# Expert loads and stores from ScalarE's queue, a second row buffer for the last batch, and two reordered table steps, in a fused transformer block on one core

## The chip, the core and the metric

One core of a Trainium2 chip runs the whole program in one launch. The engines are TensorE (PE in the rows), VectorE (DVE), ScalarE (ACT), GpSimd (POOL) and SyncE (SP, which only issues transfers here). The metric is the device time of one execution in microseconds. Three executions of the kernel before took 423.67, 422.94 and 422.52 us, median 422.94.

## The reference

The block has two halves on x of 4 batches by 512 tokens by 256 features, in float32:

```
mod = silu(c) @ wmod                       # per batch: sa, ca, ga, sb, cb, gb (256 each)
ga, gb = sign * max(|.|, 0.25)
h = layernorm(x) * (1 + ca) + sa
q, k, v = h @ wq + bq, h @ wk + bk, h @ wv + bv          # 16 heads of 16
scores = (q k^T) * gamma**(n - m) for n >= m, else 0      # retention, no softmax
ret = scores @ v, normed per head over (tokens, features), * gn_w + gn_b
x = x + ga * ((silu(h @ wg + bg) * ret) @ wo + bo)
h = layernorm(x) * (1 + cb) + sb
top 2 of 8 experts by h @ gate; weights = softmax over the two
x = x + gb * sum over the two of weight * (silu(h @ w0[e]) * (h @ w1[e])) @ wo[e]
```

Each expert has two 256x512 matrices and one 512x256. All outputs are returned as 4x512x256.

## The kernel before, in words

**Attention half.** A loop over the four batches (b = 0 to 3), unrolled, is written out once for each engine. For batch b TensorE does the projections q0, q1, k0, k1 (`project`), the value rows v01 and v23 (`rows_v`), the transposed keys (`rows_k`), the gate g0 and g1, the chunk states (`state_parts`), the scores of two sets of chunks (`scores(b, 0)` and `scores(b, 1)`), the products with the states (`from_states`), and transposes the next batch's x (`turn_x`). ScalarE takes results out of PSUM (`queries`, `keys`, `gate`, `features`), and VectorE masks the scores (`masks`) and adds. The second product with the values (`values(b, u)`) runs one batch later, between the projections. So do the per-head norm (`average`, `group_stats` to `group_scale`, `group_normed`), the product with the gate (`gated`), the output projection (`out_rows`, `attention_out`), the second layernorm (`second_normed`, written to the row buffer h2) and its transposes (`turn_h2`, `h2_features`). The router (`router`), its ranking (`rank`, `choose_top` to `rows_of_tokens`) and GpSimd's `scatter` of each token's row to DRAM run two batches later. Eight indirect transfers of 260 KB a batch write each token's row (features, weights, token number, gb) to the place of its two experts in `routed`.

PSUM results go through two rings. The front ring has four banks, so item i may be written when item i - 4 is drained: scores s03 of the last batch needs the bank of g0. The tail ring has two banks, with logits, rank, the table steps and the outputs in a fixed order of `tail_items`.

**Expert half.** 39 tiles of 128 rows, each of one expert. Tiles 0 to 8 (`EARLY`) hold rows of the first two batches alone and start while the last batch is still in its tail. Their table (which tile begins where, of which expert) is made in the last batch by `tiles_of_experts(0)`, `counts(0)`, `tiles_before(0)`, `firsts(0)`, `tile_columns(0)`, `fold(0)` and `table_rows(0)`. A second table for tiles 9 to 38 is made between tiles 4 and 8. Per tile TensorE does `turn_rows`, two products up (L1657 in the early tiles, L1666 to L1670 with split weights in the later ones), `turn_hidden` (L1678) and the product down (L1686), and GpSimd adds the rows to the output in DRAM (L633).

**Order and queues.** Every engine's instructions are in an order written by hand, and every cross-engine dependency is a semaphore. SP issues nearly all transfers in its own order: at the start the inputs, then per batch the two experts of that batch (`load_expert`, three transfers of 512 KB each) behind the end of `values(b - 1, 1)` (`pv_done`), the store of x of an earlier batch (`store_x`), ga, sb and cb rows, and the gb rows into h2 (`fill_gb`, which waits for the scatter of the batch before). In the tail `second_normed(3)` on ScalarE writes to the same h2 that the scatter of batch 2 reads, and waits for it (`scattered`), and `fill_gb(3)` on SP does too. The names on the rows: `h` is h2, `parts` holds q and the states, `kT` the keys, `sm` the masked scores and also ro and the tanh, `vx` the values with zeros between heads, `we` all eight experts' weights.

The lines below are those of the profile.

Of the kernel before, what the change touches and what calls it, by code (L numbers as in the profile page):

```python
# [21 lines left out]
F32 = mybir.dt.float32  # L22
F32R = mybir.dt.float32r
I32 = mybir.dt.int32
# [101 lines left out]
def adaln_block(nc, x, wq, bq, wk, bk, wv, bv, wg, bg, wo, bo, gn_w, gn_b, gamma,  # L126
                gate_k, w0, w1, wo_e, c, wmod, out):
    ctx = ExitStack()
    with ctx:
# [75 lines left out]
        h2 = sb("h2", [P, NC, ROW])  # L205
# [4 lines left out]
        tmpl = z[:, :, :].rearrange("p k n -> p (k n)")[:, 0:ROW]  # L210
# [4 lines left out]
        zeros, idch = h2[:, 0, 0:CH], h2[:, 1, 0:CH]  # L215
# [161 lines left out]
        def _(sp):  # L377
# [3 lines left out]
            def load_expert(e):  # L381
                for o, w, k, n in we_v:
                    sp.dma_start(we[:, e, o:o + k * n].rearrange("p (k n) -> p k n", k=k),
                                 w[e].rearrange("(k p) n -> p k n", p=P)).then_inc(we_in, 16)

# [28 lines left out]
            def store_x(b, done_sem):  # L414
                wait(sp, tail.drains(b, "wo23"))
                sp.dma_start(out_v[b], xs[:, b * NC:(b + 1) * NC, :]).then_inc(done_sem, 16)

            def fill_gb(b):

                if b:  # L420
                    sp.wait_ge(scattered, SCATTERS * b)
                sp.dma_start(h2[:, 0, GB:ROW], gb_dram[b].partition_broadcast(P)).then_inc(gb_rows, 16)


            for b in range(B):
                p = b - 1
                if b == 0:
                    sp.wait_ge(front.full, front.filled(b, "q0"))
                else:
                    sp.wait_ge(pv_done, SETS * b)  # L430
                if b == B - 1:
                    sp.wait_ge(gb_out, 16)
                load_expert(2 * b)
                load_expert(2 * b + 1)
                if p >= 0:
                    sp.wait_ge(front.full, front.filled(b, "g0" if b == B - 1 else "g1"))
                    if p >= 1:
                        store_x(p - 1, x2_out)
                    if b + 1 < B:
                        sp.wait_ge(x1_ready, b)  # L440
                        load_ga(b + 1)
                    if p >= 1:
                        sp.wait_ge(h2_ready, p)
                        load_sbcb(p)
                    fill_gb(p)
# [1325 lines left out]
```

## Time and profile before

| | |
|---|---|
| median of three executions | 422.94 us |
| profiled execution, its own time | 424.81 us |
| its span, first to last instruction | 423.1 us |
| mean granted TensorE clock | 0.937 |
| TensorE busy | 373.8 us (88%) |
| VectorE, ScalarE, GpSimd busy | 257.2, 171.5, 229.5 us |
| moved by DMA | 49.05 MB, mean 116 GB/s |

The span is what the rows speak of, and the rest of the profiled time lies around it. Busy time of TensorE is modelled from the issue of matmuls, so a granted clock of 0.5 shows as longer matmuls and not as idle time. The attention half takes about 172 us, the overlap of its tail with the early tiles goes on to about 250, and the rest is the loop over tiles.

### The profile page before, as it was taken

To read this page: it belongs to the slowest core of one execution; us is meant where nothing else is said; L and a number is where in the kernel's file an instruction comes from. 1 tells how busy PE (TensorE), PEld (TensorE's weight loads), DVE (VectorE), ACT (ScalarE), POOL (GpSimd) and SP (SyncE) were. 2 spreads that over 40 slices of the span, in tenths; PEclk is the share of its full clock that TensorE was granted. 3 is DMA by queue.
4 is the path that set the end of the run, shared out by engine and by line. 5 is a ranking of instruction groups with operands and counts; after the bars stand their busy time and mean duration, and the time that the engine had idled before them with its cause. 6 is when DMAs were issued, how large, how long until landed. Compare 5 with 4: busy or idle time off the path is not lost.

```text
span 423.1 us, 11448 instructions
## 1 busy us (share of the span) xinstructions
PE 373.8 (88%) x3889; PEld 278.0 (66%) x3890; DVE 257.2 (61%) x726; ACT 171.5 (41%) x262; POOL 229.5 (54%) x172
## 2 busy tenths in 40 slices
PE   3995899999889859887799899999999999999990
PEld 3464657776666537654476468888888888888870
DVE  6368317836833658673265566777777777777740
ACT  3514145463444311221331145555555555555530
POOL 3202520563754253617256457787777778777751
PEclk9998589999968988999699999999999999999997
DMA  6819007007900884217229844433333433433322
GB/s 226 273 34 317 4 24 279 28 2 258 323 24 3 282 294 119 52 52 252 53 42 285 245 84 75 78 75 75 75 75 75 75 75 75 75 75 76 51 25 25
DMA packets 32322, 49.05 MB, mean 116 GB/s; under 512 B 3198, under 2 KB 18972, under 8 KB 32284
## 3 DMA queue, kind: packets, MB, share of 16 engines
q1 hardware_dynamic: 23656, 34.60, 27.4%
q0 software_dynamic: 8176, 13.65, 14.6%
q8 instruction: 26, 0.43, 0.4%
q10 hardware_dynamic: 452, 0.28, 0.2%
q14 instruction: 12, 0.10, 0.1%
HBM read 30.35 MB, written 18.16 MB: 115 GB/s over the span
## 4 chain that ended last, share of the span: by engine, by line
PE 67%; issue 8%; DVE 8%; ACT 4%; DMA 4%; POOL 3%; SPq 2%; POOLq 0%; ACTq 0%; DVEq 0%
PE ps L1686 14%; PE ps L1391 9%; PE ps L1670 6%; PE ps L1667 6%; PE ps L1666 6%; PE ps L1678 3%; PE ps L1505 3%; PE ps L1657 3%; PE ps L1410 3%; PE ps L1444 2%; PE ps L1480 2%; DMA out_dram<-wg_s,qd 2%; POOL routed L591 2%; PE ps L1573 2%; PE ps L1465 1%
## 5 line engine op out<-in xcount | busy, mean ns | idle before, releaser
L623 POOL TENSOR_TENSOR w_lo<-we,w_hi 128x1024 fp32r<-128x1024 f32 x30 | 74.7, 2490 | 20.7 <-ACT w_hi L807 20.5
L1686 PE MATMUL ps<-we,qeo 128*128 x312 | 77.7, 393 | 6.6 <-ACT qeo L792 6.2
L1686 PEld LDWEIGHTS ps<-we,qeo 128*128 128x128 f32 x312 | 58.2, 193 | 25.1 <-issue 17.7
L633 POOL DMA_INDIRECT out_dram<-wg_s,qd x30 | 47.1, 1570 | 38.8 <-issue 15.8
L792 ACT COPY qeo<-ps 128x512 f32<-128x512 f32 x39 | 22.9, 586 | 105.1 <-PE ps L1678 105.1
L591 POOL DMA_INDIRECT routed<-h,idx x32 | 33.0, 1031 | 20.1 <-DVE idx L1131 11.2
L1292 DVE TENSOR_TENSOR w_halves<-we,w_halves 128x1024 fp32r<-128x1024 f32 x30 | 36.8, 1226 | 7.6 <-ACT w_halves L807 7.6
L1657 PE MATMUL ps<-we,xn 128*128 x72 | 36.5, 632 | 0.8 <-issue 0.8
L1272 DVE SCALAR_TENSOR_TENSOR sm<-sm,ps 128x512 f32<-128x512 f32 x39 | 26.5, 679 | 12.7 <-ACT sm L797 12.7
L1264 DVE CAST rT_halves<-ps 128x256 fp32r<-128x256 f32 x30 | 12.7, 424 | 33.2 <-PE ps L1573 33.2
L807 ACT CAST w_hi<-we 128x1024 fp32r x30 | 31.6, 1053 | 0.0
L807 ACT CAST w_halves<-we 128x1024 fp32r x30 | 31.4, 1048 | 0.2 <-issue 0.2
L1666 PE MATMUL ps<-w_halves,rT_halves 128*128 128x512 f32 x60 | 29.2, 487 | 0.0
L1279 DVE TENSOR_TENSOR sm<-sm,ps 128x512 f32<-128x512 f32 x39 | 26.5, 680 | 0.4
L1666 PE MATMUL ps<-w_hi,rT_halves 128*128 128x512 f32 x60 | 26.1, 435 | 0.0
L1017 DVE TENSOR_TENSOR sm<-ps,dmask 128x512 f32<-128x512 f32 x32 | 19.8, 681 | 9.1 <-PE ps L1444 9.1
L1678 PE MATMUL ps<-ident,sm 128*128 128x128 f32 x156 | 23.5, 273 | 0.3 <-DVE sm L1279 0.3
L736 ACT ACTIVATE h<-xs,nmr,rs 128x256 f32<-128x256 f32 x16 | 8.3, 590 | 37.9 <-POOL nmr L535 20.7
L1667 PE MATMUL ps<-w_halves,rT_halves 128*128 128x512 f32 x60 | 23.6, 394 | 0.0
L1667 PE MATMUL ps<-w_hi,rT_halves 128*128 128x512 f32 x60 | 23.6, 394 | 0.0
L797 ACT ACTIVATE sm<-ps 128x512 f32<-128x512 f32 x39 | 23.6, 604 | 0.0
L1678 PEld LDWEIGHTS ps<-ident,sm 128*128 128x128 f32 x156 | 19.1, 140 | 6.7 <-issue 2.1
(228 smaller groups left out, 725.2 us busy)
## 6 DMA issues: line engine op xcount, KB each, us to landing
rowbuf<-routed SPq DMA_DIRECT2D x39, 260.5 KB, 2.9
we<-in_ffn_w_kernel_dram SPq DMA_DIRECT2D x16, 512.0 KB
we<-in_ffn_wo_kernel_dram SPq DMA_DIRECT2D x8, 512.0 KB
routed<-z SPq DMA_DIRECT2D x9, 260.5 KB, 3.9
xs<-in_attn_x_dram SPq DMA_DIRECT2D x4, 512.0 KB, 11.7
out_dram<-xs SPq DMA_DIRECT2D x4, 512.0 KB, 3.1
we<-in_wmod_dram SPq DMA_DIRECT2D x1, 1024.0 KB, 10.0
sbcb<-gsc_dram SPq DMA_DIRECT2D x4, 256.0 KB, 5.8
```

Of the source, the lines that this page charges most:

```text
L591: g.indirect_dma_start(routed, bass.IndirectOffsetOnAxis(ap=idx[:, k, t:t + 1], axis=0), h2[:, t, :], None).then_inc(scattered, 16)
L623: g.tensor_tensor(w_lo[1], expert_up(e, 1), w_hi[1].bitcast(F32), ALU.subtract)\
L633: g.indirect_dma_start(out, bass.IndirectOffsetOnAxis(ap=meta[s % 4][:, TOK - D:TOK - D + 1].bitcast(I32), axis=0), ey[s % 2], None, compu ...
L807: a.copy(w_hi[which], expert_up(e, which)).then_inc(w_hi_ready[which], 1)
L1272: v.scalar_tensor_tensor(out=eth[s % 2], in0=eth[s % 2], scalar=1.0, in1=up_ps[s % 2][0][:, :], op0=ALU.add, op1=ALU.mult).then_inc(in_don ...
L1292: v.tensor_tensor(w_lo[0], expert_up(e, 0), w_hi[0].bitcast(F32), ALU.subtract)\
L1391: last = mm(front.bank(b, n)[:, :], s[:, k, ft * P:(ft + 1) * P], hT[:, k, :], start=k == 0, stop=k == FT - 1)
L1657: last = mm(up_ps[s % 2][which][:, :], rT[s % 2][:, k, :], weights(e, (which * FT + k) * F, F), start=k == 0, stop=k == FT - 1)
L1666: mm(dst, rT_hi[s % 2][:, k, :], w_hi[which][:, k * F:(k + 1) * F], start=k == 0, stop=False)
L1667: mm(dst, rT_lo[s % 2][:, k, :], w_hi[which][:, k * F:(k + 1) * F], start=False, stop=False)
L1678: last = tr(ps[5][:, k * P:(k + 1) * P], ein[s % 2][:, k * P:(k + 1) * P], ident[:, :])
L1686: last = mm(down_ps, eit[s % 2][:, k, :], weights(e, 2 * FT * F + k * D, D), start=k == 0, stop=k == KF - 1)
```

## The change

1. `load_expert` and `store_x` leave SP's queue and go to ScalarE's. Experts 0 and 1 are issued behind `keys(0, 1)`. In batch b >= 1 expert 2b is issued behind `queries(b, 0)` and expert 2b + 1 behind `keys(b, 0)`, with no wait for `pv_done`. `store_x(p)` is issued ahead of `h2_features(p)`, and that of batch 3 behind `act_step(2, 2)`.
2. The last batch gets a row buffer of its own, `h2_last`, at the address of vx (and the first 36 elements of z). `second_normed(3)` and `fill_gb(3)` no longer wait for `scattered`. `fill_gb(3)` moves up behind the loads of tile 1's rows. A wait for all scatters is new ahead of the first split weights (`weights_hi(9)`), which are written over vx, and `gb_copies(3)` waits for `prod_ready`.
3. In the last batch TensorE's `counts(0)` goes behind the projection k1, and VectorE's `tiles_before(0)` behind `group_stats`.
4. VectorE's `tile_columns(0)` goes ahead of `gated`.

```diff
@@ buffers
-        h2 = sb("h2", [P, NC, ROW])
+        h2_first = sb("h2_first", [P, NC, ROW])
+        h2_last = nc.alloc_sbuf_tensor_at("h2_last", [P, NC, ROW], F32, offset=offset["vx"])
+        spill = (NC * ROW - 2 * NC * D)
+        tmpl = z[:, :, :].rearrange("p k n -> p (k n)")[:, 2 * spill:2 * spill + ROW]
+        h2 = [h2_first, h2_first, h2_first, h2_last]
...
@@ SP
             def fill_gb(b):
 
-                if b:
+                if b == B - 1:
+                    sp.wait_ge(pv_done, SETS * B)
+                elif b:
                     sp.wait_ge(scattered, SCATTERS * b)
...
-            for b in range(B):
+            for b in range(1, B):
                 p = b - 1
-                if b == 0:
-                    sp.wait_ge(front.full, front.filled(b, "q0"))
-                else:
-                    sp.wait_ge(pv_done, SETS * b)
-                if b == B - 1:
+                sp.wait_ge(pv_done, SETS * b)
+                if b + 1 < B:
+                    sp.wait_ge(x1_ready, b)
+                    load_ga(b + 1)
+                if p >= 1:
+                    sp.wait_ge(h2_ready, p)
+                    load_sbcb(p)
+                if p == 0:
                     sp.wait_ge(gb_out, 16)
-                load_expert(2 * b)
-                load_expert(2 * b + 1)
...
@@ SP, early tiles
                 if i == 1:
-                    store_x(B - 2, x2_out)
                     sp.wait_ge(h2_ready, B - 1)
                     load_sbcb(B - 1)
-                if i == 3:
-                    store_x(B - 1, x2_last)
-                if i == 4:
                     fill_gb(B - 1)
@@ ScalarE
                 act.wait_ge(shift2, b + 1)
-                if b:
+                if 0 < b < B - 1:
                     act.wait_ge(scattered, SCATTERS * b)
...
                 queries(b, 0)
+                if b == B - 1:
+                    act.wait_ge(gb_out, 16)
+                if b:
+                    load_expert(2 * b)
                 if p >= 1:
                     top_tanh(p - 1)
...
                 keys(b, 0)
+                if b:
+                    load_expert(2 * b + 1)
                 keys(b, 1)
+                if b == 0:
+                    load_expert(0)
+                    load_expert(1)
...
+                    store_x(p)
+                if p >= 0:
                     if p == 0:
                         act.wait_ge(mod2_ready, 2)
                     h2_features(p)
...
             act_step(2, 2)
+            store_x(b)
             h2_features(b, [0])
@@ VectorE
                         tiles_of_experts(0)
+                    group_stats(p)
+                    if last:
                         tiles_before(0)
-                    group_stats(p)
...
                 rows_v(b, "v23", 2)
+                if last:
+                    tile_columns(0)
                 if p >= 0:
                     gated(p)
@@ TensorE
                     values(p, 1)
+                project(b, "k", wk_s, 1)
                 if final:
                     counts(0)
-                project(b, "k", wk_s, 1)
```

Three places where the instructions of an engine stand otherwise. The first is VectorE in the last batch, from the last value rows to the chunk states; `sm<-sm,z` is the product with the gate, `stc` to `done` the tile columns. Before:

```order
L967 TENSOR_TENSOR vx<-ps,bv_bc 128x8x2x16 x2
L1056 TENSOR_TENSOR sm<-sm,z 128x512 x2
L1168 TENSOR_SCALAR stc<-ps 8x1
L1174 TENSOR_TENSOR enc<-stc,tls 8x1
L1175 SCALAR_TENSOR_TENSOR bas<-stc,base 8x1
```

and after, with the tile columns' last operation directly ahead of the gate product:

```order
L1175 TENSOR_SCALAR stc<-ps 8x1
L1181 TENSOR_TENSOR enc<-stc,tls 8x1
L1182 SCALAR_TENSOR_TENSOR bas<-stc,base 8x1
L1184 TENSOR_SCALAR tile_i<-tile_f,stc 8x39
L1185 SCALAR_TENSOR_TENSOR bas<-done,bas 8x1
L1187 SCALAR_TENSOR_TENSOR ine<-tile_f,enc,tile_i 8x39
L1189 TENSOR_SCALAR row<-tile_f,bas 8x39
L1190 TENSOR_TENSOR tab<-row,ine 8x39
L1191 TENSOR_SCALAR tab<-ine,ecol 8x39
L1194 TENSOR_SCALAR done<-stc 8x1
L1195 SCALAR_TENSOR_TENSOR done<-done,tls 8x1
L1063 TENSOR_TENSOR sm<-sm,z 128x512 x2
```

All eleven operations of the tile columns are now ahead of the two gate products.

The second is ScalarE in the last batch, from the queries of tile 0 to the keys of tile 1 (with the waits at the rows' ends). Before:

```order
L694 ACTIVATE parts<-ps,vcol 128x512 [waits front_full]
L696 ACTIVATE qeo<-ps,bqp,par 128x8x64 x2
L745 ACTIVATE vt<-vd 128x4 [waits vd_ready]
L694 ACTIVATE parts<-ps,vcol 128x512 [waits front_full]
L696 ACTIVATE qeo<-ps,bqp,par 128x8x64 x2
L702 ACTIVATE kT<-ps,vcol 128x512 [waits front_full] x2
```

and after:

```order
L679 ACTIVATE qeo<-ps,bqp,par 128x8x64 x2
L730 DMA we<-in_ffn_w_kernel_dram 128x2x512 [waits gb_out]
L730 DMA we<-in_ffn_w_kernel_dram 128x2x512
L730 DMA we<-in_ffn_wo_kernel_dram 128x4x256
L739 ACTIVATE vt<-vd 128x4 [waits vd_ready]
L677 ACTIVATE parts<-ps,vcol 128x512 [waits front_full]
L679 ACTIVATE qeo<-ps,bqp,par 128x8x64 x2
L685 ACTIVATE kT<-ps,vcol 128x512 [waits front_full]
L730 DMA we<-in_ffn_w_kernel_dram 128x2x512 x2
L730 DMA we<-in_ffn_wo_kernel_dram 128x4x256
L685 ACTIVATE kT<-ps,vcol 128x512 [waits front_full]
```

Six transfers stand between activations that PSUM banks wait for.

The third is ScalarE at the early tiles 1 and 2, where `h` is the row buffer, L797 the tanh of a tile and L792 the copy of its hidden rows. Before:

```order
L797 ACTIVATE sm<-ps 128x512 [waits in_done,up0_full]
L736 ACTIVATE h<-xs,nmr,rs 128x256 [waits scattered,shift2]
L736 ACTIVATE h<-xs,nmr,rs 128x256 x3
L792 COPY qeo<-ps 128x512 [waits dn_full,it_full]
L797 ACTIVATE sm<-ps 128x512 [waits in_done,up0_full]
L727 ACTIVATE hT<-ps,modT 128x512 [waits tail_full]
```

and after:

```order
L802 ACTIVATE sm<-ps 128x512 [waits in_done,up0_full]
L719 ACTIVATE h_last<-xs,nmr,rs 128x256 [waits shift2]
L719 ACTIVATE h_last<-xs,nmr,rs 128x256 x3
L797 COPY qeo<-ps 128x512 [waits dn_full,it_full]
L802 ACTIVATE sm<-ps 128x512 [waits in_done,up0_full]
L735 DMA out_dram<-xs 128x4x256 [waits tail_dve]
L710 ACTIVATE hT<-ps,modT 128x512 [waits tail_full]
```

The order of the activations is the same, the wait for `scattered` is gone from the norm, and the store of batch 3 is new.

## Rows read from the trace of the kernel before

**Rows 1.** Windows table; busy us of each engine, clock, DMA share, GB/s.
```profile
38.00:42.00 4.00, 2.21 (x90) 1.79 (x76) 3.62 (x7) 0.00 (x0) 0.80 (x2) 0.56 0.95 330
114.00:118.00 4.00, 0.86 (x55) 0.72 (x49) 3.72 (x11) 0.00 (x0) 3.18 (x4) 0.87 0.63 218
151.00:157.00 6.00, 1.63 (x72) 1.32 (x64) 2.67 (x8) 0.00 (x0) 3.94 (x4) 0.80 0.89 305
...
204.00:210.00 6.00, 6.00 (x13) 3.73 (x14) 1.86 (x3) 0.14 (x1) 0.96 (x1) 0.57 0.22 61
```
**Rows 2.** Chain of waits; start us, us, what.
```profile
40.21 3.25 issue
...
114.78 3.14 issue
...
152.49 4.37 issue
...
170.79 0.69 issue
```
**Rows 3.** Windows between restarts; columns of rows 1 (matmuls, weight loads first).
```profile
43.45:117.92 74.46, 68.77 (x1394) 49.40 (x1395) 41.81 (x132) 31.12 (x52) 33.70 (x30) 0.89 0.39 132
117.92:130.44 12.52, 11.93 (x253) 10.03 (x253) 3.99 (x19) 7.09 (x12) 7.92 (x5) 0.76 0.05 14
130.44:156.84 26.41, 19.42 (x380) 12.57 (x379) 14.94 (x65) 7.20 (x12) 10.67 (x11) 0.89 0.66 222
156.84:167.87 11.02, 10.53 (x253) 8.34 (x254) 8.40 (x22) 0.95 (x2) 2.23 (x3) 0.79 0.45 134
167.87:171.47 3.61, 2.71 (x128) 2.21 (x127) 0.89 (x2) 2.57 (x5) 3.39 (x4) 1.00 0.02 5
```
**Rows 4.** The page's DMA queues; packets, MB, share.
```profile
q8 instruction: 26, 0.43, 0.4%
```
**Rows 5.** Timeline of SP's queue; start us, us, line.
```profile
30.03 0.94 SPq L383 DMA_DIRECT2D we<-in_ffn_w_kernel_dram  x2
...
137.96 1.76 SPq L383 DMA_DIRECT2D we<-in_ffn_w_kernel_dram  x2
...
148.85 0.39 SPq L416 DMA_DIRECT2D out_dram<-xs  x1
```
**Rows 6.** Expert loads by line (ns min/median/max), then ScalarE's timeline with its idle time.
```profile
L383 SPq DMA_DIRECT2D we<-in_ffn_w_kernel_dram x16: 368/489/1475, 30.0 to 140.8; - x16
...
31.90 0.69 ACT L708 ACTIVATE z<-ps,vcol 128x512 f32<-128x512 f32 x1 [8.34 <-PE ps L1391]
...
134.48 0.69 ACT L694 ACTIVATE parts<-ps,vcol 128x512 f32<-128x512 f32 x1 [4.57 <-PE ps L1391]
```
**Rows 7.** Timeline of the last batch; start us, us, instruction [idle before <-releaser].
```profile
139.17 0.20 PE L1545 MATMUL ps<-ident,carry_early 128*8 128x1 f32 x2 [1.24 <-DVE base L1142]
...
149.33 0.14 DVE L1168 TENSOR_SCALAR stc<-ps 8x1 f32<-8x1 f32 x1
149.45 0.69 ACT L708 ACTIVATE z<-ps,vcol 128x512 f32<-128x512 f32 x1 [1.79 <-DVE sm L1056]
...
149.62 1.48 PE L1426 MATMUL ps<-vx,xn 64*32 64x32 f32 x112 [0.80 <-DVE stc L1168]
...
151.55 0.15 DVE L1188 SCALAR_TENSOR_TENSOR done<-done,tls 8x1 f32<-8x1 f32 x1
```
**Rows 8.** Timeline from the down product of tile 0 on.
```profile
192.41 1.89 PE L1686 MATMUL ps<-we,qeo 128*128 x8
...
194.03 0.20 POOL L535 TENSOR_TENSOR nmr<-nm,rs 128x4 f32<-128x4 f32 x1
...
201.10 2.07 ACT L736 ACTIVATE h<-xs,nmr,rs 128x256 f32<-128x256 f32 x4 [9.35 <-DMA routed<-h,idx]
...
203.80 3.78 PE L1686 MATMUL ps<-we,qeo 128*128 x8 [5.42 <-ACT qeo L792]
...
207.37 2.77 PE L1657 MATMUL ps<-we,xn 128*128 x4
```

More of the change, by code:

```diff
@@ L412, in _ @@
             load_ga(1)
-            def store_x(b, done_sem):
-                wait(sp, tail.drains(b, "wo23"))
-                sp.dma_start(out_v[b], xs[:, b * NC:(b + 1) * NC, :]).then_inc(done_sem, 16)
             def fill_gb(b):
-                if b:
+                if b == B - 1:
+                    sp.wait_ge(pv_done, SETS * B)
+                elif b:
                     sp.wait_ge(scattered, SCATTERS * b)
-                sp.dma_start(h2[:, 0, GB:ROW], gb_dram[b].partition_broadcast(P)).then_inc(gb_rows, 16)
-            for b in range(B):
+                sp.dma_start(h2[b][:, 0, GB:ROW], gb_dram[b].partition_broadcast(P)).then_inc(gb_rows, 16)
+            for b in range(1, B):
                 p = b - 1
-                if b == 0:
-                    sp.wait_ge(front.full, front.filled(b, "q0"))
-                else:
-                    sp.wait_ge(pv_done, SETS * b)
-                if b == B - 1:
-                    sp.wait_ge(gb_out, 16)
-                load_expert(2 * b)
-                load_expert(2 * b + 1)
[L435 to L445, printed above, removed]
+                sp.wait_ge(pv_done, SETS * b)
[6 more added lines that the diff above has]
+                if p == 0:
+                    sp.wait_ge(gb_out, 16)
+                fill_gb(p)
             def load_rows(i, s):
@@ L740, in gb_copies, with load_expert, store_x @@
                 act.wait_ge(gb_rows, 16 * (b + 1))
-                a.copy(h2[:, 1:NC, GB:ROW], h2[:, 0:1, GB:ROW].broadcast_to([P, NC - 1, D])).then_inc(gb_copied, 1)
+                if b == B - 1:
+                    act.wait_ge(prod_ready, FT * B)
+                a.copy(h2[b][:, 1:NC, GB:ROW], h2[b][:, 0:1, GB:ROW].broadcast_to([P, NC - 1, D])).then_inc(gb_copied, 1)
+            def load_expert(e):
+                for o, w, k, n in we_v:
+                    act.dma_start(we[:, e, o:o + k * n].rearrange("p (k n) -> p k n", k=k),
+                                  w[e].rearrange("(k p) n -> p k n", p=P)).then_inc(we_in, 16)
+            def store_x(b):
+                wait(act, tail.drains(b, "wo23"))
+                act.dma_start(out_v[b], xs[:, b * NC:(b + 1) * NC, :]).then_inc(x2_last if b == B - 1 else x2_out, 16)
             def top_tanh(b):
@@ L1237, in _ @@
                     first_stats(1)
-                if last:
-                    tile_columns(0)
                 states(b)
@@ L1514, in turn_h2 @@
                     for t in range(NC):
-                        last = tr(tail_bank(b, n)[:, t * P:(t + 1) * P], h2[:, t, ft * P:(ft + 1) * P], ident[:, :])
+                        last = tr(tail_bank(b, n)[:, t * P:(t + 1) * P], h2[b][:, t, ft * P:(ft + 1) * P], ident[:, :])
                     last.then_inc(tail.full, 1)
```

21 lines of the change are left out of this document (9 added, 12 removed).

## The prediction, made before the changed kernel was run

> **What bounds the kernel now.** I read the page first for the shape: TensorE is busy 88% of the span and granted a mean clock of 0.937, so no other engine is near the bound, and what can be won is time in which TensorE stands still or runs at half its clock. Then the windows table, which says where that is. In three stretches of 4 to 6 us TensorE is busy for a fifth to somewhat over a half of the time, 38 to 42 and 114 to 118 in the middle of the attention part and 151 to 157 in the last batch; a fourth, 204 to 210, is busy throughout but at a granted clock of 0.57, near the lower level of 1.2 GHz (0.5) [rows 1]. That one follows a wait of 5.4 us that ends at 203.80 [rows 8]. The second half (expert tiles from about 250 us on) is a steady loop of about 5.3 us a tile with TensorE busy throughout. The change leaves that loop alone, so I look for the shift at which the loop is entered.
>
> The chain of waits shows what the first three stretches are: pieces called "issue" of 3.25, 3.14 and 4.37 us, in which TensorE waited for nothing that the profile shows [rows 2]. Each lies within a run of like small matmuls (from_states or scores), whose waits are all at its first instruction. A fourth such piece, 0.69 us, lies in values(3, 1). The counts between them say what they have in common: from one restart to the next TensorE issued 1394+1395, 253+253, 380+379, 253+254 and 128+127 matmuls and weight loads, each a little short of 11, 2, 3, 2 and 1 times 256 [rows 3] (a few per cent of records and the other instructions make up the rest). So TensorE stops at the end of a fixed-size block of its program and goes on when the next block is there. The page has a DMA queue for instructions, 26 packets with 0.43 MB, 16.5 KB a packet [rows 4]: the blocks come over the same 16 DMA engines as the data. Where the DMA share was 0.95, 0.63 and 0.89 [rows 1] the piece was 3.1 to 4.4 us, and where it was 0.02 it was 0.7 us [rows 2, 3]. I take the block's packet to stand behind whatever transfers are already queued. The Trainium skill (Runtime: NRT & Kernel Launch, Instruction fetch mechanics) says that instructions are refilled in 16 KiB blocks of 256 by a DMA queue of the sequencer, and that the cost of a boundary is "mostly hidden". The trace agrees on the block; the "mostly hidden" it contradicts at these three places, and by that rule the change would win nothing there (rival B).
>
> What was queued then is in SP's own order: expert weights, 3 MB a batch, from 30.03 and again from 137.96, and a 512 KB store of x at 148.85 [rows 5]. Batches 1 and 2 have the like.
>
> **The change, part by part.** Sums are made against the profiled execution: span 423.1, run 424.81, which is 1.87 above the median of 422.94. I subtract the sum from the median.
>
> (1) Experts 0 and 1 move from SP, behind the modulation rows, to ScalarE behind keys(0, 1). ScalarE has then nothing to do for 8.34 us (its next activation is at 31.90) [rows 6]. Six issues by 0.49 us, the median, are 2.9 us, and by the longest, 1.475, 8.9 us [rows 6]: hidden in all but the worst case, which would add 0.5. The 3 MB start at about 23.6 instead of 30.0, and are over at about 34 or 35 instead of 42 at this case's 350 to 380 GB/s. TensorE's next dense run starts at 37.2, so the stop of 3.25 us at 40.21 goes: gain 3.3. What is late next is the half clock, granted from 38.5 to 55 before. It came with the idle 34.3 to 37.1, which stays. I price it at nothing, and a faster return at up to 2.2 more (3.8 us of q0 projection at half speed). Lower end of this part: 0.
>
> (2) In batches 1 to 3 each expert is issued behind queries(b, 0) or keys(b, 0), and the x stores of batches 0 to 2 one stage later. That is 18 loads and 3 stores in ScalarE's order. Behind a load wait queries(b, 1), keys(b, 1) and the tanh for the weights. ScalarE sits idle 4.57 us before queries(3, 1) [rows 6], and in other batches the gaps there are 2 us or a little more, against three issues of 0.5 to 0.8 us each, so I cost it at nothing, up to 2 us in all. The second stop (3.14, batch 2): experts 4 and 5 now start some 6 and 3 us earlier and the store is gone from 109, so only the scatter of batch 0, paced by GpSimd at 1.27 us a piece, is left in flight. The stop shrinks to the uncongested 0.7 or less: gain 2.7. With no clock drop behind it (0.5 to 123.7) the 64 scores matmuls and eight transposes that took half speed come back by about 1: I take 0.6 of it. Sum 3.3, ends 0 and 4.5.
>
> (3) Last batch. counts(0) moves behind the k1 projection: TensorE's wait of 1.24 us for VectorE [rows 7] is covered by the projection, and VectorE starts the group statistics 0.9 us earlier without the four operations of tiles_before, so that average(2) comes 0.8 earlier: gain 0.8. tile_columns(0), from 149.33 to 151.70, 2.37 us [rows 7], now stands ahead of the gating product. So the firsts column is drained 1.8 us earlier, and state_parts doesn't wait its 0.80 us. But gate(3, 0) on ScalarE, which waits for the product (1.79 us already) [rows 7], starts 2.4 us later, and scores(3, 0) need its bank. They begin at about 153 instead of 151.1. That is where the stop of 4.37 us was: by then the experts (issued from 129 and 137 instead of 138) are over and the store is gone, so the block is there. scores end at 154.3 instead of 157.5. Then VectorE is late next: the table's rows, the gate product and four masks (some 3.9 us in all) end at 158.2, and the residual sum behind them, held by out_rows at half clock until 161.65 before, starts 3.4 earlier. TensorE, which comes to values(3, 0) early, runs into the block period that the trace shows undisturbed, 3.61 us from 167.87 to 171.47 [rows 3]: boundaries at 159.6, 163.2 and 166.8 instead of 164.8, 167.87 and 171.47, so values(3, 1) end 4.6 earlier. I take 4.2, between VectorE's 3.4 and TensorE's 4.6; ends 1.0 (if the stop stays) and 6.
>
> (4) The last batch's rows get a buffer of their own. second_normed(3) no longer waits for the scatter of batch 2, only for shift2, ready at 194.24 instead of 201.10 [rows 8]. turn_back(1) follows it, so ScalarE copies at 196.5 instead of 203.08. TensorE's down(1) then starts when its own projection ends, 198.4 instead of 203.80: 5.4. Without the idle the clock doesn't fall: down(1) takes 1.89 instead of 3.78, and the 2.77 of the next up part 1.88, 2.4 together up to the transposes at 209.98 [rows 8]. SP no longer waits for the scatter before fill_gb(3), so row 5 comes earlier. What is late next is GpSimd: its first accumulation lands at about 205 and the fifth tile's meta copy needs it, which costs at most 1. The new store sits in front of h2_features, 0.4 us, while ScalarE waits. The new wait of the first split weights for all scatters comes 9 us behind the last of them and is hidden. Gain 7.4, ends 4 and 8.1.
>
> Sum: 3.3 + 3.3 + 4.2 + 7.4 = 18.2, so 422.9 - 18.2 = 404.7; I say 405.
>
> A second rule of the Trainium skill speaks against (1) and (2): DMA: Bandwidth & Descriptors, "Issuing engines are not separate DMA queues", says that DMAs of all engines share the same 16 and that another issuer only saves issue time. The rows agree in that SP's issues cost nothing here: what is won is not by the other queue but by the earlier start.
>
> **Rivals.**
> A, the forecast: about 405 (399 to 410).
> B, the stops stay or move. If the block packets are late for another reason, or the expert bursts now catch the blocks fetched under values(0, 1) and values(1, 1), only (4) and the reorder of (3) remain. For it: the burst of batch 1 starts within a microsecond of a block boundary (11 blocks lie between 43.45 and 117.92), and 1.5 MB take 4.5 us. Against it: the boundaries after that have 5 us or more to the next. Time: 422.9 - 7.4 - 1.0 = 414.5, and 411 to 418 with one of the stops gone.
> C, the late gate decides. scores(3, 0) wait so long that the clock falls and out_rows stays slow, and GpSimd is the bound after 205. Part 3 gives 1, part 4 gives 5: 422.9 - 3.3 - 3.3 - 1 - 5 = 410.3, in A's or B's range.
> D, slower. ScalarE's queue blocks. If the ring is full, each of the 22 issues (18 loads, 4 stores) in its order takes the longest time seen on SP, 1.48 us, and all of it lies on the path of queries, keys and gates: 32.6 - 18.2 = 14.4, so 437. It decides above 18.2 / 22 = 0.83 us exposed per issue. For it: on SP the second load of a burst took that long. Against: idle of over 4 us beside most of them.
> E, the change doesn't do what it says: second_normed(3) is held by something that comes as late as the scatter, as its shift2 is computed on GpSimd between two pairs of scatters. The trace has it at 194.24, so little speaks for it: 422.9 - 10.8 = 412.1.
>
> **Chances.** A 0.58, B 0.22, C 0.08, E 0.03, D 0.05, and 0.04 for a sum near nothing. The range that should hold 8 in 10 goes down to 399 (part 1 with the clock back, part 2 and 3 at their ends) and up to 415, which takes in C, E and most of B. 0.3% is about what a measurement of this kernel can tell from no change, 1.3 us: faster 0.92, same 0.02, slower 0.06.
>
> **What would show it.** In the windows of the changed kernel the DMA burst of the first experts lies at 24 to 35, and no "issue" piece of over 1 us is left inside from_states(0), from_states(2) and scores(3, 0). ScalarE waits less than 1 us for anything behind a load. gate(3, 0) starts about 2 us after its old place relative to the product's operands. second_normed(3) is released by GpSimd's nmr, not by a DMA, TensorE's wait before down(1) is under 1 us and the clock beside it 1.00. The tile loop keeps 5.3 us. I am wrong if an "issue" piece of 2 us or more stands in values(0, 1) or values(1, 1), or if queries(b, 1) start later than before relative to their matmul.

## The result and the profile after

The changed kernel takes 405.25 us (median of 4 executions, 403.61 to 409.28), the kernel before 423.07 (4, 422.52 to 423.67). The ratio is 0.958, 95% interval 0.952 to 0.965: 17.8 us faster, against 18.2 forecast. A later series gave 405.79 (6 executions, 402.61 to 408.86). The trace below is of the execution that took 409.28, the slowest, with a span of 407.6; the others had spans of 401.9 to 403.6, so a part of what it shows is not in all of them. The medians here take in every execution; the ratios with an interval leave out those more than 1.5% above the fastest of their kernel.

The page of the changed kernel, queues and chain by engine:

```profile
PE 366.4 (90%) x3889; PEld 271.3 (67%) x3890; DVE 259.6 (64%) x726; ACT 171.3 (42%) x262; POOL 228.9 (56%) x172
...
q10 hardware_dynamic: 11140, 14.96, 10.7%
q8 instruction: 26, 0.43, 0.4%
...
PE 72%; DVE 8%; issue 6%; DMA 4%; ACT 4%; SPq 2%; POOL 1%; POOLq 0%; ACTq 0%; DVEq 0%
```
TensorE is busy for 7 us less, ScalarE's queue (q10) carries the 15 MB of experts and stores, and the instruction queue is the same [rows 4]. The chain of waits of the changed kernel (start us, us, what; "issue" is time in which TensorE waited for nothing that the profile names) answers to [rows 2]:

```profile
40.25 1.11 issue
...
90.72 1.10 issue
...
155.40 0.85 issue
158.89 0.98 issue
```
The piece in from_states(0) has fallen from 3.25 to 1.11 us. There is a new one of 1.10 in values(1, 1), and none in scores(3, 0). TensorE's timeline (idle before in brackets) shows the stretch around the first stop, the second stop and the last batch:

```profile
37.94 1.20 PE L1452 MATMUL ps<-qeo,kT 32*64 32x128 f32 x64 [2.34 <-ACTq L696]
...
42.34 1.62 PE L1452 MATMUL ps<-qeo,kT 32*64 32x128 f32 x64
...
109.44 1.18 PE L1473 MATMUL ps<-qd,parts 32*32 32x64 f32 x60
111.40 1.06 PE L1473 MATMUL ps<-qd,parts 32*32 32x64 f32 x52 [0.79 <-issue]
...
122.18 0.66 PE L1488 MATMUL ps<-sm,vx 64*32 64x64 f32 x27 [0.57 <-issue]
...
143.73 2.02 PE L1452 MATMUL ps<-qeo,kT 32*64 32x128 f32 x64 [2.73 <-ACTq L696]
```
The stop of batch 2 is 0.79 instead of 3.14. The block restart in values(2, 0) that stood at 130.44 [rows 3] comes at 122.18. In the last batch the 64 scores matmuls run through, but TensorE waited 2.73 us for the late gate first, and the 64 took 2.02 us, against 1.20 for the same count at 37.94: they ran at a granted clock of 0.50 instead of 1.00.

Around the routed rows of the last batch (timeline, for [rows 8]):

```profile
180.45 1.89 PE L1694 MATMUL ps<-we,qeo 128*128 x8
...
182.09 0.20 POOL L518 TENSOR_TENSOR nmr<-nm,rs 128x4 f32<-128x4 f32 x1
...
182.33 2.08 ACT L719 ACTIVATE h_last<-xs,nmr,rs 128x256 f32<-128x256 f32 x4 [2.54 <-POOL nmr L518]
...
186.26 1.89 PE L1694 MATMUL ps<-we,qeo 128*128 x8
```
second_normed(3) is released by GpSimd's nmr, down(1) waits for nothing and takes 1.89 instead of 3.78. Up to here TensorE is 17.5 us ahead of before (186.26 against 203.80). Then a part is given back. These are windows from down(2) to down(12), the changed kernel's first, then those of before:

```profile
195.15:259.37 64.22, 59.80 (x252) 41.52 (x252) 40.76 (x113) 21.51 (x33) 39.37 (x25) 0.95 0.52 130
```
```profile
215.43:275.26 59.83, 57.50 (x253) 40.24 (x252) 38.50 (x113) 21.64 (x33) 35.92 (x24) 1.00 0.55 137
```
The same ten tiles take 4.4 us longer, at a mean clock of 0.95 instead of 1.00. From down(12) on the shift stays: 15.9 us there, 15.5 at the end of the span.

### The profile page after: what moved, and what is told of

Its sections match the earlier page's. It is cut to its first block, busy times and chain, and to the rows that moved or that the text cites. A ratio compares the mean times of both kernels' runs of the same rounds, so it can differ in the third digit from the quotient of the medians.

```text
span 407.6 us, 11447 instructions
## 1 busy us (share of the span) xinstructions
PE 366.4 (90%) x3889; PEld 271.3 (67%) x3890; DVE 259.6 (64%) x726; ACT 171.3 (42%) x262; POOL 228.9 (56%) x172
## 4 chain that ended last, share of the span: by engine, by line
PE 72%; DVE 8%; issue 6%; DMA 4%; ACT 4%; SPq 2%; POOL 1%; POOLq 0%; ACTq 0%; DVEq 0%
PE ps L1694 14%; PE ps L1399 10%; PE ps L1675 6%; PE ps L1674 6%; PE ps L1678 6%; PE ps L1665 5%; PE ps L1513 4%; PE ps L1686 3%; PE ps L1488 3%; PE ps L1418 3%; PE ps L1581 2%; DMA out_dram<-wg_s,qd 2%; PE ps L1531 2%; DVE sm L1024 2%; PE ps L1452 2%
## 5 line engine op out<-in xcount | busy, mean ns | idle before, releaser
L1694 PE MATMUL ps<-we,qeo 128*128 x312 | 75.9, 386 | 1.1 <-ACT qeo L797 0.8
L797 ACT COPY qeo<-ps 128x512 f32<-128x512 f32 x39 | 22.9, 587 | 109.2 <-PE ps L1686 109.0
L574 POOL DMA_INDIRECT routed<-h_first,idx x24 | 24.7, 1030 | 16.2 <-DVE idx L1138 9.4
L1399 PE MATMUL ps<-hT,wq_s 128*128 128x512 f32 x32 | 21.3, 809 | 2.0 <-ACT hT L669 1.8
L530 POOL TENSOR_TENSOR qd<-parts,qdec 128x512 f32<-128x512 f32 x8 | 9.5, 1183 | 21.1 <-ACT parts L677 21.1
```

The source lines that it names most:

```text
L1399: last = mm(front.bank(b, n)[:, :], s[:, k, ft * P:(ft + 1) * P], hT[:, k, :], start=k == 0, stop=k == FT - 1)
L1694: last = mm(down_ps, eit[s % 2][:, k, :], weights(e, 2 * FT * F + k * D, D), start=k == 0, stop=k == KF - 1)
```

## Experiments

All times are medians; the kernel before ran beside each series and had 422.59 (19 executions, 412.60 to 439.35), 421.05 (11) and 421.50 (11). With that scatter, differences between two variants under some 2 us are not settled by the medians. The traces show where a wait stands and how long it is, but each is of one execution, and two traces of the same kernel differ too. Parts are numbered as in the prediction: 1 the loads of batch 0, 2 those of the other batches and the stores, 3 the reordering, 4 the buffer. In the edits, "..." marks what is left out.

**The two halves.** Only the last batch's buffer (part 4):

```diff
-        h2 = sb("h2", [P, NC, ROW])
+        h2_first = sb("h2_first", [P, NC, ROW])
...
+        h2_last = nc.alloc_sbuf_tensor_at("h2_last", [P, NC, ROW], F32, offset=offset["vx"])
...
+        h2 = [h2_first, h2_first, h2_first, h2_last]
```

> The kernel before with only the last batch's row buffer (h2_last over the values, gb_copies and fill_gb(3) at their new places); loads, stores, counts and tile columns stand as before. Theory: the wait of second_normed(3) for batch 2's scatter (5.42 us before router(3)) goes, and with it the half clock behind it, while 1 to 4 us come back in the tile tables and row loads behind the routing: 415 to 418 us, 5 to 8 faster than before; the stops at 40, 114 and 152 us stay at 3.2, 3.1 and 4.4 us. Rival (the gain of the whole change is in the queues alone, and the wait is replaced by another one in front of router(3)): 421 to 423 us.

417.62 us, 5.0 below before, span 415.7 against 423.1. Its stops stay at 4.03, 2.86 and 3.52 us. down(2) starts at 206.81, 8.6 earlier than before, and down(12) at 267.75, 7.5 earlier. The theory holds, with 417.62 in its range of 415 to 418; about 1 us is given back here between down(2) and down(12).

Only the queues (parts 1 and 2):

```diff
-                load_expert(2 * b)
...
-                        store_x(p - 1, x2_out)
...
+                if b:
+                    load_expert(2 * b)
...
+                    store_x(p)
```

The removed lines are SyncE's, the added ones ScalarE's. With them gone, SyncE's ga, sb and cb rows come earlier too.

> The kernel before with only the expert loads and the stores moved from SyncE to ScalarE; buffer, counts and tile columns as before. Theory: stops at 40 and 114 us fall to about 1 us, a new one of about 1 us comes in values(1,1), the stop in scores(3,0) shrinks or stays at up to 4.4 us since the batch's late part is as before: 411 to 417 us, 6 to 12 faster than before. Rival (ScalarE's queue pays for the issues, about 1.5 us each where it is waited for, so the loads alone bring nothing): 420 to 425 us. Second rival (the stops depend on the place in the program, not on what lies on the DMA engines): all three stops stay at 3 to 4 us, and the time is within 1 us of before.

409.98 us, 12.6 below before in the medians; the ratio is 0.973 (0.963 to 0.982), which is 7.5 to 15.7 us. That is the upper end of the 6 to 12 expected. TensorE's timeline of this kernel:

```profile
38.06 3.33 PE L1465 MATMUL ps<-qd,parts 32*32 32x64 f32 x112
...
46.06 1.98 PE L1391 MATMUL ps<-hT,wq_s 128*128 128x512 f32 x4 [1.00 <-ACT hT L665]
...
139.65 1.42 PE L1444 MATMUL ps<-qeo,kT 32*64 32x128 f32 x61
142.70 0.43 PE L1444 MATMUL ps<-qeo,kT 32*64 32x128 f32 x3 [1.63 <-issue]
...
178.02 1.89 PE L1686 MATMUL ps<-we,qeo 128*128 x8
...
200.91 1.97 PE L1686 MATMUL ps<-we,qeo 128*128 x8
```
No stop at all in from_states(0), and the following four projection matmuls at full clock (1.98 us) where before and the changed kernel took 3.78 and 3.51. But the 112 products took 3.33 us, where the changed kernel's two pieces took 1.18 and 1.05: the clock had fallen ahead of them instead. From the first scores matmul on it was 0.60 in the mean (window):

```profile
36.68:40.90 4.22, 4.21 (x162) 3.64 (x166) 3.36 (x6) 0.00 (x0) 1.58 (x2) 0.60 0.01 4
```
 The stop in scores(3, 0), which I had given to the reordering, is already 1.63 instead of 4.37 without it. The scatter's 5.42 us wait before down(1) is there as before.

**Queue or moment.** The changed kernel with SyncE issuing the expert loads at ScalarE's moments (the stores stay on ScalarE; shown for batches 1 to 3):

```diff
+                wait(sp, front.drains(b, "q0"))
...
+                load_expert(2 * b)
+                wait(sp, front.drains(b, "k0"))
+                load_expert(2 * b + 1)
```

> The changed kernel, except that SyncE issues the expert loads, at the moments of the batch at which ScalarE issued them (it waits for the drained banks of k1 in batch 0, of q0 and k0 in the others); the stores stay on ScalarE. Theory (what counts is when the loads' bursts stand against the block fetches, and not the queue that issues them): within 1.5 us of the changed kernel, 404 to 407 us, stops as in its chain (1.1 us at 40, 1.1 us at 91). Rival (ScalarE's own queue is the gain, because SyncE keeps its loads of ga, the shift rows and gb behind the waits): 410 to 417 us, with waits for those rows. Second rival (the issues on ScalarE cost it time): 401 to 403 us.

407.38 us (402.85 to 409.50), as good as the changed kernel (402.61 to 409.28), though a little above the 404 to 407 expected; the ratio to before is 0.961 (0.949 to 0.972), against 0.958. So for the expert loads the gain is the moment, not the queue. The rule of the Trainium skill that I weighed (DMA: Bandwidth & Descriptors, "Issuing engines are not separate DMA queues") says that a transfer runs on the same DMA engines whichever engine issues it, and this run agrees. The pieces are not all those of the changed kernel's chain: the first is 2.40 us instead of 1.11, and none stands at 91. What made the first longer is looked at below.

**Is a stop a block boundary?** The kernel before with 32 more TensorE instructions in the setup (each transpose is a weight load and a matmul):

```diff
+            for _ in range(16):
+                tr(ps[6][:, 0:P], ident[:, :], ident[:, :])
```

> The kernel before with 16 extra transposes of the identity on TensorE in the setup, into a bank that is overwritten later, so that every later matmul stands 32 instructions further on in TensorE's program. Theory (a stop is TensorE waiting for its next block of 256 instructions, fetched behind the expert bursts): the stops stay in the program's rhythm, so they move 16 matmuls ahead: in from_states(0) to behind some 46 matmuls instead of 62, in scores(3,0) to behind some 45 instead of 61; lengths of 2 to 5 us as before, total 421 to 426 us. Rival (the stops belong to what stands at that place, a bank or an operand): they stay behind the same matmuls, 62 and 61.

Timeline of before (for the counts), then of the shifted kernel:

```profile
38.32 1.89 PE L1465 MATMUL ps<-qd,parts 32*32 32x64 f32 x62
43.46 1.70 PE L1465 MATMUL ps<-qd,parts 32*32 32x64 f32 x50 [3.25 <-issue]
45.09 2.92 PE L1444 MATMUL ps<-qeo,kT 32*64 32x128 f32 x64
...
151.06 1.43 PE L1444 MATMUL ps<-qeo,kT 32*64 32x128 f32 x61
156.85 0.69 PE L1444 MATMUL ps<-qeo,kT 32*64 32x128 f32 x3 [4.37 <-issue]
```
```profile
38.25 0.94 PE L1467 MATMUL ps<-qd,parts 32*32 32x64 f32 x46
39.34 1.29 PE L1467 MATMUL ps<-qd,parts 32*32 32x64 f32 x66
...
143.63 1.08 PE L1446 MATMUL ps<-qeo,kT 32*64 32x128 f32 x45
148.51 1.11 PE L1446 MATMUL ps<-qeo,kT 32*64 32x128 f32 x19 [3.79 <-issue]
```
In scores(3, 0) the stop is behind 45 matmuls instead of 61, exactly 16 ahead, and nearly as long. In from_states(0) the break is behind 46 as expected, but it is no stop any more. In from_states(2) it is behind 44 instead of 60, with 1.23 us instead of 3.14, and a stop of 2.39 us stands ahead of it at 101.60, in the gate projection. So the places follow the count of TensorE's instructions, and the lengths follow what is under way there. The Trainium skill has such a boundary "mostly hidden" (Runtime: NRT & Kernel Launch, Instruction fetch mechanics); the 3.79 us here contradict it for dense small matmuls beside full DMA engines. Total 419.20, 3.4 below before in the medians, but the ratio is 1.002 (0.985 to 1.019), so the time has not changed; I had expected 421 to 426.

The traces also hold the start and the duration of every DMA packet, and the queue q8 of [rows 4] is TensorE's: this kernel has 27 packets on it instead of 26. In the kernel before the packets run from 40.92 to 42.00, 115.46 to 116.40 and 154.56 to 155.44 us, each inside one of the three stops, and TensorE starts again 1.46, 1.52 and 1.41 us behind their ends. Between 20 and 172 us the fourteen traces have 107 "issue" pieces ahead of TensorE's matmuls: 95 of them end 1.2 to 1.6 us behind the end of such a packet. The other twelve stand ahead of an up product or of out_rows(3), 3.0 us or more behind a packet, so they are waits of another kind. The queue's rows in the DMA view of before (packets, MB, share), over 40.90 to 41.00, 115.40 to 115.50 and 154.50 to 154.60 us, in which the three packets start:

```profile
q8 instruction: 1, 0.02, 68.0%
...
q8 instruction: 1, 0.02, 58.6%
...
q8 instruction: 1, 0.02, 55.4%
```
This shows what the stops are: the packet itself takes about 1 us, as elsewhere, but it starts late. That other transfers delay its start follows from the runs in which these were moved.

How late can be read as well. Where small matmuls follow and the DMA engines are free, the next packet starts 1.05 to 1.14 us behind the block's first matmul (43.46 to 44.51, 167.87 to 168.97, 171.48 to 172.62). With 1.0 for the packet and 1.4 behind it, a block takes 3.5 us, while its 128 small matmuls take 1.5 to 2.4 at full clock. That is the period of 3.61 us in [rows 3], and a remainder of about 1 us is left in such a run even when nothing holds the packet. In the changed kernel the packet of from_states(0) starts at 39.06, 1.12 us behind the first scores matmul at 37.94, so nothing held it, and the 1.11 us left are this remainder. With the queues alone it starts 1.02 us behind (36.68 to 37.70): there the block was in time because TensorE, at the lower clock, came to the boundary later. In the run with SyncE's early loads it starts 2.27 us behind (37.62 to 39.89), and the piece is longer by about as much. In the kernel before it starts 3.72 us behind (37.20 to 40.92), in the shifted one at 36.92, ahead of the scores.

**What held the block of batch 2.** The kernel before with experts 4 and 5 loaded in batch 1:

```diff
-                load_expert(2 * b)
-                load_expert(2 * b + 1)
+                if b != 2:
+                    load_expert(2 * b)
+                    load_expert(2 * b + 1)
+                if b == 1:
+                    load_expert(4)
+                    load_expert(5)
```

> The kernel before with experts 4 and 5 loaded by SyncE right behind 2 and 3 in batch 1, and no expert load in batch 2; all else as before. Theory (the packet of the block stood behind these loads): the stop in from_states(2) falls from 3.14 to 0.7 to 1.1 us and the clock there stays full, the stops at 40 and 152 us stay over 3 us, and nothing else moves much: 417 to 421 us. Rival (the store of x and the scatter, which stay where they are, hold the packet): the stop stays at 2.5 to 3.2 us.

The rival came out, a shade above its 2.5 to 3.2 us. Timeline and a window of this kernel:

```profile
117.39 1.17 PE L1469 MATMUL ps<-qd,parts 32*32 32x64 f32 x60
121.81 1.71 PE L1469 MATMUL ps<-qd,parts 32*32 32x64 f32 x52 [3.25 <-issue]
```
```profile
114.00:120.00 6.00, 4.56 (x135) 3.71 (x134) 5.14 (x15) 1.08 (x2) 4.16 (x6) 1.00 1.02 290
```
With no expert load in batch 2 the DMA engines are still full from 114 to 120, the block's packet starts only at 119.48, and the stop is 3.25 us. SyncE issued the store of x, the ga and the shift rows there from 112.77 on, beside the scatter. Which of these transfers alone would do it was not tried. A new stop of 2.67 us stands at 81.44, behind the doubled burst of batch 1. The time is of only two executions (417.77 and 428.39) and says nothing.

**The reordering.** The changed kernel once more, then without part 3:

> The changed kernel once more, unaltered, as the yardstick for the three kernels that run beside it. 403 to 409 us as measured before, and 16 to 19 below the kernel before.

```diff
-                if last:
-                    tile_columns(0)
...
+                if last:
+                    tile_columns(0)
...
-                project(b, "k", wk_s, 1)
                 if final:
                     counts(0)
+                project(b, "k", wk_s, 1)
```

> The changed kernel without its third part: counts(0), tiles_before(0) and tile_columns(0) stand at their old places; loads and stores on ScalarE and the buffer of the last batch as changed. Theory (formed after the two halves, 5.0 and 12.6 us below before, already made up the whole gain of 17.8): the queues had already shortened the stop in scores(3,0) from 4.37 to 1.63 us, so the reordering is worth 0 to 1.5: 404 to 408 us, within 1.5 of the changed kernel beside it. Rival (the prediction's term 3 at its full size): 4 us slower than the changed kernel, 409 us. In its trace I expect an issue piece of 1.0 to 2 us in scores(3,0) and no 2.7 us wait of TensorE for the gate.

405.79 (15.3 below before, a little under the 16 to 19 expected) and 407.87: 2.1 apart in the medians, with scatters of 402.6 to 408.9 and 401.6 to 411.6. The ratios to before, 0.964 (0.958 to 0.969) and 0.965 (0.956 to 0.973), do not tell them apart, so no gain of the reordering is shown. Its two halves taken back one at a time, tile_columns(0) behind the gate first, then counts(0) ahead of k1:

> The changed kernel with tile_columns(0) back behind the gating product; counts(0) behind k1 as changed. Theory (the columns delay gate(3,0) by some 2.4 us, TensorE waits 2.7 us for it and its clock falls, while the stop that the delay was to cover is over): scores(3,0) start 2 us earlier and an issue piece of 0.5 to 2 us comes back in them, together 0 to 2 us faster than the changed kernel beside it. Rival (the earlier block boundary is worth more than the gate): 1 to 3 us slower.

> The changed kernel with counts(0) back ahead of the k1 projection and tiles_before(0) ahead of group_stats(2); tile_columns(0) stays ahead of the gating product. Theory (no reorder at all cost 2.1 us and the columns alone gave 1.0 back, so the counts are worth about 3): 407.5 to 409.5, with the 1.24 us wait of TensorE for the base back. Rival (the 3 us are scatter between executions, the counts are worth the 0.8 us of the prediction): 405.5 to 407.

404.82 and 404.87 (the second in another series): neither alone costs anything that can be seen. With the columns behind the gate a piece of 1.52 us stands in scores(3, 0) again, and the 2.73 us wait for the gate is gone, as expected. With the counts back, TensorE's wait for the base is 0.46 us and not the expected 1.24. The 3 us that I expected of the counts did not show in the time, as the rival had it. What remains of the reordering is 0 to 2 us.

**Where the last 4 us went.** Timeline of the changed kernel, SyncE and TensorE:

```profile
206.18 9.83 SPq L456 DMA_DIRECT2D routed<-z  x8
...
217.36 15.75 SPq L439 DMA_DIRECT2D rowbuf<-routed  x4
...
219.69 0.29 PE L1573 MATMUL ps<-tab,ones 8*1 8x78 f32 x2 [1.43 <-DVE tab L1191]
...
222.83 0.69 PE L1581 MATMUL ps<-ident,rowbuf 128*128 128x128 f32 x2 [1.91 <-DMA rowbuf<-routed]
...
223.31 3.62 PE L1665 MATMUL ps<-we,xn 128*128 x4
```
Tile 8's rows are the first of the four loads at 217.36, behind the eight padding writes, and TensorE waits 1.91 us for them; the clock falls to 0.50 around these two waits, and the next up part takes 3.62 instead of 1.88. Rows ahead of six of the writes:

```diff
-                    for e in range(E):
+                if i in (7, 8):
+                    for e in (range(2) if i == 7 else range(2, E)):
```

> The changed kernel, with the load of tile 8's rows issued on SyncE behind the padding writes of experts 0 and 1 and ahead of those of experts 2 to 7, instead of behind all of them (it relies on tile 8 not being the last tile of a later expert, as in these inputs). Theory (tile 8's rows land late, 1.9 us of TensorE's time, and the idle costs 2 us more at half clock): 2 to 4 us faster than the changed kernel beside it. Rival (the fold of the counts, that is VectorE and GpSimd, is late by as much, so the wait only changes its name): 0 to 1 us faster.

404.49, 1.3 below the changed kernel beside it. TensorE's wait for these rows is gone, that for the counts' table (1.39 us) stays. The medians lie between theory and rival, at the rival's end, and 1.3 us is less than they can settle.

Both single edits together:

> The changed kernel with both single edits of the last two runs: tile 8's rows ahead of the padding of experts 2 to 7, and tile_columns(0) back behind the gating product. Theory (the two cover partly the same 3.4 us, lost between the down products of tiles 5 and 6, since with the columns back that stretch was already 9.2 instead of 12.1 us): 403 to 405, 1 to 2 us below the changed kernel, no more than the better of the two alone. Rival (they add): 402 to 403.

402.22 us (398.54 to 403.60, 6 executions), 19.3 below before beside it and the fastest of all; the ratio is 0.968 (0.956 to 0.980), which rests on two executions of before. I had expected 403 to 405; the time lies in the rival's 402 to 403. Its window from down(2) to down(12), then that of the kernel with the columns alone put back:

```profile
193.39:253.56 60.17, 57.76 (x253) 40.08 (x252) 39.68 (x113) 21.75 (x33) 36.96 (x25) 1.00 0.54 136
```
```profile
197.37:257.51 60.14, 57.33 (x253) 40.45 (x252) 39.45 (x113) 21.53 (x33) 38.10 (x25) 1.00 0.55 138
```
4.1 of the 4.4 us are back in both, with the clock at 1.00, though the second still waits 1.52 us for tile 8's rows. With the rows moved alone the stretch takes 61.29 us at a clock of 0.97. So much of the 4.4 us is the fallen clock, and the row load is only one of the waits around it; the kernel without the reordering lost the clock (0.95) with a row wait of 0.93 us. What decides whether it falls there is not shown. All six executions lie below the changed kernel's median of 405.79, which ran in another series. The next wait is in this trace too: TensorE stands 3.22 us ahead of out_rows(3), against 1.19 in the changed kernel, and the gating product on VectorE ends 0.1 us before it goes on. The edit relies on tile 8 not being the last tile of expert 2 or a later one, true for these inputs and not in general.

**The shift on the changed kernel.** The same 16 transposes as above:

> The changed kernel with 16 extra transposes of the identity on TensorE in the setup, which bring all later block boundaries 16 matmuls ahead. Theory (blocks): the 1.1 us piece in from_states(0) goes, since the boundary's packet is asked for before the rows of ga and sbcb are under way; those in values(3,1) stay near 1 us but 16 matmuls ahead: 402 to 405.5. Rival (the shift only moves the pieces under another burst): 405 to 407.

409.03 us (406.43 to 412.27), 3.2 above the changed kernel of the series before: a miss for both. The piece in from_states(0) is gone as forecast, one of 0.64 us has come at 104.52, and down(0) stands at 180.41 in the trace against 180.45. That trace is of an execution of 406.51, near the lowest; where the others lost their 3 us stays open.

**The traces side by side.** When down(0) and down(12) start, and the time of the execution traced:

| kernel | down(0) | down(12) | its time |
|---|---|---|---|
| before | 192.41 | 275.26 | 424.81 |
| buffer alone | 192.10 | 267.75 | 417.38 |
| queues alone | 178.02 | 260.14 | 410.07 |
| changed | 180.45 | 259.37 | 409.28 |
| changed again | 180.95 | 259.02 | 408.86 |
| no reordering | 183.51 | 261.79 | 411.61 |
| both single edits | 178.68 | 253.56 | 403.34 |

The two traces of the changed kernel agree within 0.5 us. But the queues alone reach down(0) 2.4 us ahead of the whole change, and without the reordering it is 5.5 us later, so a part's term of a few us can't be read off two such rows.

## Why the prediction held, step by step

The total was right (405 against 405.25), and so was the mechanism of the stops. The terms were not: parts 1 and 2 brought some 12 us instead of 6.6, part 3 brought 0 to 2 instead of 4.2, and part 4 brought less on top of the others than the 7.4 forecast. That the errors cancel to 0.4 us is luck. The prediction also took 0.3% for what a measurement of this kernel can tell; the 41 later executions of the kernel before spread over 412.5 to 439.4 us.

*Part 1, forecast 3.3 (0 to 5.5).* In the changed kernel the four projection matmuls of batch 1 start at 47.11 instead of 50.84, 3.7 earlier, though its setup happened to be 0.7 later; in its second trace they start at 47.77. The stop gave 2.1 and not 3.3, since 1.1 is left. The prediction had the fetch period of 3.61 us in hand and used it for part 3 alone; here it would have given the remainder. The rest is the clock: the 64 scores matmuls behind the stop took 1.62 us instead of 2.92. The clock was not kept, as the 3.51 us of the projection show. It fell at about 47 instead of 38.5 and was back at about 50 instead of 55, and in the second trace it was low from about 43 to 53.

```profile
50.84 3.78 PE L1391 MATMUL ps<-hT,wq_s 128*128 128x512 f32 x4 [0.87 <-ACT hT L686]
```
```profile
47.11 3.51 PE L1399 MATMUL ps<-hT,wq_s 128*128 128x512 f32 x4 [1.00 <-ACT hT L669]
```
The first line is of before, the second of the changed kernel. ScalarE hid the six issues: the next activation had waited 8.34 us for TensorE, as before [rows 6], and its loads took 487 ns in the median.

*Part 2, forecast 3.3.* From q0(1) to the block restart in values(2, 0) the lead grew from 3.7 to 8.3 us (130.44 to 122.18), that is 4.5. The size is at the upper end of the range given (0 to 4.5). The reason was half wrong: I put the stop mainly to experts 4 and 5, and their removal alone left 3.25 us. The later store and SyncE's earlier ga and shift rows took the other transfers away from there, and the prediction had not counted those rows.

*Part 3, forecast 4.2 (1 to 6).* This step failed in size: 0 to 2. I read the stop of 4.37 us as the reordering's to remove. But by the queues alone it was 1.63, since experts 6 and 7 and the store no longer lay on the block. So 2.7 us belonged to parts 1 and 2, whose 6.6 became 12.6 in the medians, and what the reordering then took from the stop it gave back in the wait for the gate (2.73 us and a lower clock), which rival C had named. The block's packet ran inside that wait (141.11 to 142.18): the piece was covered by a longer one.

*Part 4, forecast 7.4 (4 to 8.1).* The mechanism is shown: nmr releases, down(1) is 17.5 us ahead, 5.6 more than down(0). Alone it moved down(12) by 7.5. On top of the queues it gave less: from down(0) to down(2) the changed kernel takes 14.7 us where the queues alone took 22.9, which is 8.2, but most of it is lost by down(12): from down(0) to down(12) it is 78.9 us against 82.1 with the queues alone and 82.9 before. So 3 to 4 us of the forecast 7.4 are left in this trace, at or under the lower end of 4. The prediction had "costs at most 1" there, with GpSimd as the late one. It was waits for the table and for the row load behind the padding writes, and the clock that fell beside them.

*Rivals.* B did not decide, though a trace of it is there (1.10 us in values(1, 1)), under the 2 us that I had set. D's price was too high: an issue on ScalarE took 0.49 us and hid beside idle time. E fell with the nmr release.

*What the trace was to show.* One bound was missed narrowly, with the piece of 1.11 us in from_states(0). The wait of 2.73 us ahead of scores(3, 0) had no bound. ScalarE's gate waited 4.04 us for the product instead of 1.79, the 2 us later that were forecast. The clock beside down(1) was 1.00, and the tile loop kept 5.3 us.

## What to carry to other kernels

In this kernel an "issue" piece inside a run of like matmuls was TensorE waiting for the next block of its program. Three things told it: the counts of instructions between restarts, the shift by 16 matmuls, and an instruction packet that ended 1.2 to 1.6 us before each restart. An "issue" piece ahead of the first instruction of a group can be a wait of another kind. Where the packet starts late, look at everything on the DMA engines in that window (stores, broadcasts, scatters), since the largest load need not be the one that holds it. Expect the piece to shrink to what the fetch takes anyway, about 1 us in a run of small matmuls here, and not to nothing. When several edits bear on one stop, its length can be won only once: run each alone before giving it a term. And after a wait of several us is gone, look for the load that is now behind a batch of writes on its queue, and for the clock beside it.

## What was not expected of the hardware

Two small operations of VectorE took long while GpSimd ran large products. Timeline of the changed kernel around the routing:

```profile
194.47 2.74 POOL L541 TENSOR_TENSOR h_last<-h_last,sbcb 128x1024 f32<-128x1024 f32 x1
...
195.97 1.27 DVE L1091 TENSOR_TENSOR vd<-mx 128x4 f32<-128x4 f32 x1
...
197.83 1.67 DVE L1097 CAST ixf<-ix 128x8 f32<-128x8 uint32 x1
```
A difference of 4 columns takes 1.27 us and a cast of 8 columns 1.67 while GpSimd's large products run; the same cast took 0.17 us in the kernel before, where it came behind them. Both end 0.03 us behind the GpSimd product they overlap (197.24 behind 197.21, 199.50 behind 199.47). The same difference ends 0.02 us behind the second product in the kernel before (0.55 us, to 216.79), with the queues alone (0.56, to 202.28) and with both single edits (1.68, to 195.89). So they ended only when GpSimd's product had ended, while other VectorE operations in the same stretch, such as four MAX8 in 0.37 us, did not wait. No experiment took the two engines apart.

The 41 executions of the kernel before that ran beside the experiments had mean clocks from 0.967 at the lowest time, 412.5 us, to 0.831 at the highest, 439.4. Without experts in batch 2 the doubled burst of batch 1 also slowed SyncE's issues: 3.66 us for two that take 1 us elsewhere.
